# Class token of the image stage in four column tiles, its weights turned once, its value added where the sums are turned

## The reference, cut to what matters

```python
h = concat([cls_tok, edges(image)])                 # 257 x 256 per image
u, v, q, k = split(silu(layernorm(h) @ W1 + b1), 4) # each 257 x 256, 16 heads of 16
scores = q @ k.T                                    # per head, 257 x 257
attn = silu(scores) / S
av = attn @ v                                       # 257 x 256
h = h + layernorm(av * u) @ W2 + b2
```

## Time and profile before

| what | value |
|---|---|
| median of 3 runs | 1697.09 us (1688.34 to 1697.24) |
| the profiled execution | 1695.56 us, its span 1693.7 us |
| TensorE busy with matmuls | 1430.5 us (84%), 12411 records |
| VectorE, ScalarE, GpSimd busy | 1074.1 us (63%), 906.9 us (54%), 423.8 us (25%) |
| image stage, one step (start of score 0 to the next) | 25.84 us at 421.95 us |

### The profile page before, as it was taken

How to read it: one execution, slowest core, us unless ns; L and a number is a source line. 1 busy time by engine, 2 the same in 40 slices (tenths; PEclk the granted TensorE clock), 3 DMA queues, 4 the chain that set the end, 5 groups by cost and what they waited for, 6 DMA issues and landing times. The chain is left out here.

```text
span 1693.7 us, 34587 instructions
## 1 busy us (share of the span) xinstructions
PE 1430.5 (84%) x12411; PEld 1158.3 (68%) x12411; DVE 1074.1 (63%) x2987; ACT 906.9 (54%) x1594; POOL 423.8 (25%) x370
## 2 busy tenths in 40 slices
PE   2499999999999999999998623326999999999997
PEld 1267676666767667667765523325889999999996
DVE  3246665666556566566655367685777777777773
ACT  0177766666666666666665203423445555555552
POOL 0011211212121121112211000002445555554553
PEclk8699999999999999999999555557999999999999
DMA  3532433424334242424300323002556556555652
GB/s 118 138 98 71 124 105 82 119 68 123 97 90 110 77 118 71 121 70 116 98 28 32 120 78 3 1 0 71 154 149 182 167 150 182 181 159 158 183 153 24
DMA packets 128692, 177.38 MB, mean 105 GB/s; under 512 B 19966, under 2 KB 116996, under 8 KB 124484
## 3 DMA queue, kind: packets, MB, share of 16 engines
q1 hardware_dynamic: 111172, 154.49, 31.1%
q0 software_dynamic: 17408, 21.25, 7.7%
HBM read 134.28 MB, written 41.41 MB: 104 GB/s over the span
## 5 line engine op out<-in xcount | busy, mean ns | idle before, releaser
L612 ACT ACTIVATE at<-ps_s 128x1024 f32<-128x1024 f32 x256 | 248.8, 1028 | 40.4 <-PE ps_s L499 37.9
L195 PE MATMUL ps_s<-xet,whi 128*128 128x322 f32 x640 | 207.1, 324 | 17.9 <-issue 10.9
L1748 POOL DMA_INDIRECT out_rows<-ye,slot_token x96 | 151.2, 1575 | 229.7 <-ACT ye L1606 218.3
L196 PE MATMUL ps_s<-xet,wlo 128*128 128x322 f32 x640 | 201.3, 315 | 0.0
L197 PE MATMUL ps_s<-xet,whi 128*128 128x322 f32 x640 | 199.8, 312 | 0.0
L1575 ACT ACTIVATE sg<-ps_s 128x322 f32<-128x322 f32 x160 | 70.5, 440 | 171.1 <-PE ps_s L197 171.0
L1670 DVE TENSOR_TENSOR wlo<-raw,whi 128x640 fp32r<-128x640 f32 x192 | 157.0, 818 | 1.3 <-ACT whi L1585 1.3
L499 PE MATMUL ps_s<-q,k 32*128 32x256 f32 x2048 | 149.6, 406 | 0.0
L195 PEld LDWEIGHTS ps_s<-xet,whi 128*128 128x128 f32 x640 | 122.4, 191 | 26.0 <-issue 26.0
L195 PE MATMUL ps_av<-whi,hs 128*128 128x256 f32 (+1 forms) x480 | 135.2, 282 | 2.9 <-DVE wlo L1670 2.9
L516 PE MATMUL ps_av<-at,uv 128*16 128x257 f32 x2048 | 136.0, 383 | 0.0
(11 more groups left out here) (350 smaller groups left out, 3529.9 us busy)
## 6 DMA issues: line engine op xcount, KB each, us to landing
raw<-in_wexp SPq DMA_DIRECT2D x32, 1280.0 KB, 6.2
halo<-gray_dram SPq DMA_DIRECT2D x96, 288.0 KB
xb<-in_x SPq DMA_DIRECT2D x64, 384.0 KB, 4.8
raw<-in_wexp SPq DMA_DIRECT2D x32, 640.0 KB, 6.1
gray_dram<-g SPq DMA_DIRECT2D x32, 256.0 KB, 3.3
out_rows<-h SPq DMA_DIRECT2D x64, 128.0 KB, 6.4
token_rows<-xf SPq DMA_DIRECT2D x64, 128.0 KB, 3.6
pre_dram<-pre SPq DMA_DIRECT2D x32, 128.0 KB, 5.1
```

Source lines behind the costliest of these rows:

```text
L195: nc.tensor.matmul(o, lh, rh, start=first, stop=False)
L196: nc.tensor.matmul(o, ll, rh, start=False, stop=False)
L612: nc.scalar.activation(at[:, t, 2 * i:2 * i + 2, :, 0:R].rearrange("p j k q -> p (j k) q"), ps_s[i][:, :, :, :].rearrange("p j k q -> p (j ...
L1748: nc.gpsimd.indirect_dma_start(out=out, out_offset=bass.IndirectOffsetOnAxis(ap=slot_token[0:w, 3 * m + st:3 * m + st + 1], axis=0), in_=y ...
```

## The change

Four edits, which belong together.

1. **Scores in column tiles.** `cls_scores` writes four tiles of 128 rows x 32 columns into the partitions of bank E: the key's scores for heads 0 to 7 in partitions 0 to 31 and for heads 8 to 15 in 32 to 63 (one product each), the query's scores in 64 to 95 and 96 to 127 (two products each, for the even and the odd heads' k). Now the class query's weights stand (32 columns, `cw`), and k moves (256 columns). So the query's scores come out with heads on partitions.
2. **A turn for the query's scores.** ScalarE takes silu of the whole bank (`clf`, 128 x 256) and of its first 64 partitions (`cls_s`, now two buffers). A new piece `cls_turn`, behind score 1, waits for that and turns the query's part by two products with `clf` standing (128 columns) and 16 selecting columns moving, into `ps_av[1]`; ScalarE copies the 32 columns to `at` after it has done silu of score 1, and weighted 0 waits for this copy.
3. **The class value is added in `back`.** The four products of 258 columns in `weighted` are gone. `back` starts each of its two banks with one product of `cls_s` (64 rows, 128 tokens standing) with `vc` (512 columns moving), and adds the turned sums.
4. **Because they add, the eight transposes are now products** with the identity (f32, not in transpose mode).

In the set-up the two `ps_av` banks are zeroed, the constants are 208 columns narrower, and `vc` has 64 rows in place of 96. The built program gives the tiles: 128 x 32 for the six products of edit 1, 128 x 128 for `cls_turn` and for the identity products, and 64 x 128 for the two products with `vc`.

```diff
@@ set-up, VectorE
+                dve.wait_ge(su_pool, 2)
+                for t in range(2):
+                    nc.vector.memset(ps_av[t][:, :], 0.0)
...
@@ TensorE
                 bank_free(pe, n, "E")
                 for a in range(2):
-                    nc.tensor.matmul(bank("E")[0:96, 0:256], kc[:, a, 0:96], q2[r % 2][:, a, :], start=a == 0, stop=a == 1)
-                mine = bank("E")[:, 256:288].rearrange("p (e a j k) -> p a k e j", e=2, a=2, j=4)
-                for a in range(2):
-                    for kt in range(2):
-                        for e in range(2):
-                            last = nc.tensor.matmul(mine[:, a, kt], k2[r % 2][:, e, a, kt * 128:kt * 128 + 128], qc[:, a, :],
-                                                    start=e == 0, stop=e == 1)
+                    nc.tensor.matmul(bank("E")[32 * a:32 * a + 32, 0:R], cw[:, a, :], q2[r % 2][:, a, :], start=True, stop=True)
+                for e in range(2):
+                    for a in range(2):
+                        last = nc.tensor.matmul(bank("E")[64 + 32 * a:96 + 32 * a, 0:R], cw[:, 2 + a, :], k2[r % 2][:, e, a, :],
+                                                start=e == 0, stop=e == 1)
                 last.then_inc(cls_ps, 1)
+
+            def cls_turn(m):
+
+                pe.wait_ge(cls_act, m + 1)
+                wait(pe, av_out, 4 * m)
+                mine = ps_av[1][:, 320:352].rearrange("p (c k) -> p k c", k=2)
+                for kt in range(2):
+                    last = nc.tensor.matmul(mine[:, kt], clf[:, kt * 128:kt * 128 + 128], cst[:, CSE:CSE + 16], start=True, stop=True)
+                last.then_inc(clt_ps, 1)
...
                 if t == 0:
-                    pe.wait_ge(cls_ready, m + 1)
+                    pe.wait_ge(clt_out, m + 1)
                     pe.wait_ge(uv_act, 2 * m + 2)
...
-                nc.tensor.matmul(o[:, 0:AW], vc[:, t, :], cls_s[:, :], start=True, stop=False, skip_group_check=True)
...
                 bank_free(pe, n, u)
+                nc.tensor.matmul(bank(u)[:, :], cls_s[(r - 1) % 2][:, hf * 128:hf * 128 + 128], vc[:, :], start=True, stop=False,
+                                 skip_group_check=True)
                 for t in range(4):
-                    last = nc.tensor.transpose(bank(u)[:, 128 * t:128 * t + 128], avs[:, t, hf * 128:hf * 128 + 128], ident)
+                    last = nc.tensor.matmul(bank(u)[:, 128 * t:128 * t + 128], avs[:, t, hf * 128:hf * 128 + 128], ident,
+                                            start=False, stop=t == 3, skip_group_check=True)
...
                     cls_scores(n, r, c)
                     score(n, r, c, 1)
+                    cls_turn(c)
                 if has(d):
-                    back(n, d, 0)
-                    back(n, d, 1)
+                    back(n, r, d, 0)
+                    back(n, r, d, 1)
@@ ScalarE
                     act.wait_ge(cls_ps, c + 1)
+                    wait(act, clt_ps, c)
+                    wait(act, cls_ready, c)
+                    wait(act, avt_ps, 2 * (c - 1))
+                    nc.scalar.activation(clf[:, :], bank("E")[:, 0:R], ACT.Silu)
+                    nc.scalar.activation(cls_s[r % 2][:, :], bank("E")[0:64, 0:R], ACT.Silu).then_inc(cls_act, 1)
+                    silu_scores(1)
+                    act.wait_ge(clt_ps, c + 1)
                     wait(act, av_ps, 4 * c)
-                    wait(act, cls_ready, c)
-                    nc.scalar.activation(cls_s[:, 0:R], bank("E")[0:96, 0:256], ACT.Silu)
-                    nc.scalar.activation(clc[64:96, :], bank("E")[64:96, 0:256], ACT.Silu)
-                    nc.scalar.activation(at[:, :, :, :, R].rearrange("p t j k -> p (t j k)"), bank("E")[:, 256:288], ACT.Silu).then_inc(cls_act, 1)
-                    silu_scores(1)
+                    nc.scalar.activation(at[:, :, :, :, R].rearrange("p t j k -> p (t j k)"), ps_av[1][:, 320:352], ACT.Copy).then_inc(clt_out, 1)
@@ VectorE
                     dve.wait_ge(cls_act, c + 1)
-                    nc.vector.tensor_tensor(cls_s[64:96, 0:R], clc[64:96, :], cls_s[64:96, 0:R].bitcast(f32),
-                                            ALU.subtract).then_inc(cls_ready, 1)
+                    nc.vector.scalar_tensor_tensor(cls_s[r % 2][:, :], cls_s[r % 2][:, :].bitcast(f32), cst[0:64, CLC:CLC + 1], clf[0:64, :],
+                                                   ALU.mult, ALU.add).then_inc(cls_ready, 1)
```

More of the change, by code:

```diff
@@ L47 @@
 CMK = CSH + 96
-CMV = CMK + 256
+CMV = CMK + 32
 CBE = CMV + 512
@@ L63 @@
 CE2 = CQM + 8
-NC_ = CE2 + 2
+CLV = CE2 + 2
+CLC = CLV + 1
+CSE = CLC + 1
+NC_ = CSE + 16
 def constants(nb):
@@ L74, in constants @@
             c[[HB * dx + r + dy for dx in range(3)], CSH + dy * 32 + r] = 1
-    for a in range(2):
+    for copy in range(3):
+        c[p, CMK + 8 * copy + p // 16] = 1
+    for h in range(H):
         for copy in range(3):
-            c[p, CMK + a * 128 + copy * 32 + 8 * a + p // 16] = 1
-    for h in range(H):
-        for s in range(3):
             at = CMV + (h % 2) * 256 + (h // 2) * 32
-            c[s * 32 + h, at:at + DH] = 1
+            c[32 * (h // 8) + 8 * copy + h % 8, at:at + DH] = 1
+    c[p % 32 // 8 == 1, CLV] = -1
+    c[p % 32 // 8 == 2, CLC] = -1
+    for e in range(2):
+        for a in range(2):
+            for j in range(4):
+                c[64 + 32 * a + 4 * e + j, CSE + 8 * e + 4 * a + j] = 1
     for j in range(4):
@@ L161, in build @@
         bias2 = s1("bias2", [P, D])
-        kc = s1("kc", [P, 2, 128])
-        qc = s1("qc", [P, 2, 8])
+        cw = s1("cw", [P, 4, 32])
         bk4 = s1("bk4", [P, 4])
-        cls_s = s1("cls_s", [96, AW], f32r)
+        cls_s = [s1(f"cls_s{i}", [64, R], f32r) for i in range(2)]
         clsav = s1("clsav", [P, 4, NB])
-        vc = s1("vc", [96, 4, 128], f32r)
+        vc = s1("vc", [64, 512], f32r)
         uvc = s1("uvc", [P, 512])
@@ L336, in _ @@
                 for a in range(2):
-                    last = nc.tensor.matmul(ps_av[1][0:32, 0:16], qkcf[:, a, :], kc[:, a, 0:16], start=a == 0, stop=a == 1)
+                    last = nc.tensor.matmul(ps_av[1][0:32, 8 * a:8 * a + 8], qkcf[:, a, :], cw[:, a, 0:8], start=True, stop=True)
                 last.then_inc(su_pe, 1)
@@ L516, in weighted, with back @@
                         last = nc.tensor.matmul(o[32 * j:32 * j + 16, 0:R + 1], uv[r % 2][:, kt, 256 + h * 16:256 + h * 16 + 16],
-                                                at[:, t, j, kt, 0:R + 1], start=False, stop=kt == 1, skip_group_check=True)
+                                                at[:, t, j, kt, 0:R + 1], start=kt == 0, stop=kt == 1)
                 last.then_inc(av_ps, 1)
-            def back(n, d, hf):
+            def back(n, r, d, hf):
                 u = ("D0", "D1")[hf]
```

25 lines of the change are left out of this document (13 added, 12 removed).

## The result

| | before | changed |
|---|---|---|
| median, same chip | 1697.16 us (4 runs, 1688.34 to 1697.97) | 1713.0 us (4 runs, 1711.36 to 1714.55) |
| profiled execution, its span | 1695.56, 1693.7 us | 1711.36, 1709.6 us |
| ordinary step | 25.77 to 25.84 us | 26.44 to 26.49 us |

The changed kernel is slower by 1.0% (ratio 1.0102, 95% interval 1.0074 to 1.0129). The forecast was 1721 with its own range 1710 to 1731, so the result lies inside it, 3 us above its lower end. The sign came out, and so did the mechanism within a step; the loss is 15.8 us by the medians and 15.9 by the spans of the profiled executions, where 24.9 were forecast.

What follows compares the result with a forecast made beforehand. TensorE's order was taken to bound each step: +1.11 us up to the q projection and -0.33 in `weighted`, times 31, plus 0.7 set-up, gave 24.9 and 1721 us. Its own range was 1710 to 1731, the overall range 1699 to 1742.

Steps and rivals of the forecast that it cites:

- The wait at score 1: Score 0 to score 1: score 1 waits for ScalarE's silu, starting at 3.22; saves 1.58 of a possible 1.72 us.
- `cls_turn`: Behind score 1: the turn waits for two ScalarE activations, starts at 4.37, and `back` starts at 5.00 us instead of 5.88.
- The four changes of shape: In `back`: changing into and out of the 64 x 128 tile, twice a step, costs 0.76 us.
- The identity products: In `back`: identity products need two records each, 0.112 us apart; the doubled records cost 0.9 us a step.
- L511 and the cover of `uvp`: In `weighted`: four L511 go, saving 0.33 us, not 0.48, because two lie where VectorE's `uvp` is dense.
- The sum: Whole kernel: 31 steps of 1.11 - 0.33 us make 24.2, plus 0.7 once for set-up, 24.9 us slower.
- 1: In `back`: changes of shape into the 64-row tile are free or nearly so; +1 us, 1698; chance 0.12.
- 2: In `back`: the `vc` product runs beside the identity products; -0.44 us a step, 1683; chance 0.05.
- 3: In `back`: identity products pay load and product one after the other, 0.22 us a record; 1774; chance 0.07.
- 4: At `cls_turn` or B0: ScalarE's longer chain adds a wait of 0.3 to 0.8 us; 1730 to 1746; chance 0.10.

Runs made afterwards that it cites:

- the kernel with the full tile: The changed kernel with the class value's operands padded with zeros from 64 to 96 rows: 1688.57 us, ratio 0.9962 to the kernel before.
- the second pair: The changed kernel and the kernel before, each profiled again without a change: 1712.14 us (ratio 1.0097) and 1696.71 us (ratio 1.0006).
- the kernel with the addition alone: The kernel before with the class value added in `back` and identity products, on 96-row tiles, class scores as before: 1729.63 us, ratio 1.02.

## Why the prediction was right, step by step

In us behind score 0, or as a length:

| step of the prediction | forecast | measured |
|---|---|---|
| score 1, waiting for silu of score 0 | 3.22 | 3.21 |
| `cls_turn` | 4.37, with a wait | 4.29, without |
| first `vc` product | 5.00 | 4.84 |
| first half of `back` to the second | 1.51 | 1.51 |
| identity records apart | 0.112 | 0.112 |
| q projection | 8.60 (+1.11) | 8.45 (+0.97) |
| q projection to the next score 0 | 18.0 | 18.03 |
| step | 26.6 (+0.78) | 26.48 (+0.64) |

- **The wait at score 1** came as forecast: score 1 starts 1.59 earlier than before, of the 1.72 that the column tiles could give.
- **`cls_turn` was mis-sized**, by 0.16. The prediction let it wait for two activations from 3.04 + 0.50 on. ScalarE starts `clf` at 3.52 as forecast, but `cls_s` only 0.26 behind it, not 0.39, and ends at 4.16; TensorE comes at 4.29. Behind it the first `vc` product follows 0.54 later, not 0.63. The drain of 0.09 is there (0.54 against 0.46 in the kernel with the full tile, four records and nothing else), but the 0.10 that the forecast put behind the row's start for a first load isn't: the second record follows the first after 0.13. Where that load went is not shown.
- **The four changes of shape**, forecast 0.76, measured 0.66 as the difference to the full tile. This was the term that no row of before could show, and it is what makes the changed kernel slower rather than equal. The Trainium skill, "TensorEngine Tiling (Array Packing)", section "Tiling Modes", lists 64 x 128 as a mode of its own and says that a change of mode drains TensorE. The runs agree that these changes are paid, with 0.66 us for four, of which a part is the bare first load.
- **The identity products**, forecast 0.9, measured 0.96. The choice between 0.055 and 0.22 a record rested on L488, whose records have the same full load and 8 columns moving; 0.112 came out exactly. By the other page of the Trainium skill that was weighed, "TensorE: Matmul & The Clock Gate", section "Terms" (transpose mode four times faster for FP32), they would have cost an estimated 2.6 a step: the runs say twice as many records at the same pace, not four times.
- **L511 and the cover of `uvp`.** Forecast -0.33 of a possible 0.48. The stretch from the q projection to the next score 0 fell from 18.35 to 18.03, and the wait for `uvp` stands where it was placed: the bank comes free 0.22 late. Only moving `uvp` gave that back: in that run the stretch is 17.80, and the whole 0.49 is saved there.
- **The sum is the term that was mis-sized**, by 9.0 us. The forecast was 31 x 0.78 + 0.7 = 24.9. Against it: steps of 0.64, 31 x 0.14 = -4.3. The zeroing of the two banks (1.02 us) did not delay the image stage, whose first turn of `xn` comes 0.8 earlier (0.2 in the second pair): -1.5. The two filling steps hold the class scores once and no `back`, and lose 1.6 where two steps of 0.64 would add 1.3: -2.9. The drain, where three `back`s stand against two class scores, +4.7 (an estimate from the step's own parts gives 3 x 2.00 + 2 x 0.55 - 2 x 1.59 - 2 x 0.32 = 3.3, the second pair 2.7), and the end +0.6. The gaps of the turns -1.4 and, in this pair, the low clock -4.3. Together -9.1, by the first pair of profiles alone; in the second pair the low clock has no part and the end has -3.1, so the split between these two is of that execution and not of the kernel. 31 equal steps were too plain a model of a pipeline with two steps that fill it, a drain and five gaps.
- **Rivals.** 1 is false as a statement on the hardware and true of the kernel with the padded tile. 2 is false: the first identity record starts 0.42 behind the `vc` record, and 0.32 in a full tile (its sum, -0.44 x 31 + 0.7, gives 1684 and not 1683). 3 is false, 0.112 and not 0.22. 4 found no place: `cls_turn` did not wait, and B0 waited the 0.22 that the forecast already had, where the rival wanted 0.3 to 0.8 more.

**What stays open:** why the clock falls behind some gaps and not behind others, why some kernels see less of the low clock than others, and the up to 3 us by which the time from the class stage to the end differs between executions of one kernel.

## What to carry to other kernels

When a change has a part that gains and a part that pays, build each alone: here the first is worth 2.1% and the second costs 2%, and together they look like a small loss. Where a product stands between full tiles, try it in a full tile: padding 64 rows to 96 with zeros gave back 24 us here. Turning a transpose into an exact product because it can then add is dear: it doubles its records, and here that alone costs 28 us, to save four products worth at most 0.49 a step. And when TensorE gets shorter, look at once for who stands just behind it: silu of the scores and VectorE's `uvp` each took back part of the gain.

## What the runs showed of the hardware

- A product in a tile of 64 x 128 between full ones: by the starts, 0.42 to the next product and 0.21 behind the last record before it, and 0.21 from the next product's first record to its second; against 0.32, 0.03 and 0.11 with 96 rows, both for 512 columns.
- The product with 96 rows shows no such distances on either side (1.13 from one `vc` product to the next, as a sum of 0.24 and eight times 0.112): here it ran as a full tile does.
- An exact (f32) product of a 128 x 128 load with 128 columns moving: two records, 0.112 apart; a transpose of the same block is one record, and the next starts 0.11 later. Records with the same load and only 8 columns moving are 0.112 apart as well (L488, kernel before), so that these rows don't tell whether the load or the product sets the pace.
- At the end of a turn of the loop TensorE stands 2.6 to 3.2 us (in the kernel with the addition alone twice 4.3 to 4.6), and behind it the granted clock is at 1.2 GHz for 3.4 or 6.8 us in some turns and not at all in others. A stretch of 3.4 us behind a gap made its step 1.3 to 1.6 us longer, one of 6.8 us 2.4 to 3.0.
